# A decoder layer on one Trainium2 core: early bounds on ScalarE, the second head's weights loaded early, the weight-sum product inside pair 3, the last row's tiles stored apart

## What is computed

```python
# 1. attention with decay: 16 heads of 128, q, k, v = split(silu(x @ Wqkv.T))
out = per head: (q k^T * decay(i - j), for i >= j) @ v        # slope per head
out = out * rsqrt(mean(out * out) + eps) * norm_w
y = (sigmoid(x @ Wg.T) * out) @ Wo.T
x = layernorm(x + y)
# 2. WKV recurrence over time, with keys x and values ctx_2048
x = layernorm(x + wkv(time_decay, time_first, x, ctx))
# 3. feed-forward with ternary weights
w_hat = sign(round(w / (mean(|w|) + eps))) * mean(|w|)         # for w_fc and w_proj
h = gelu(bitlinear(x, w_fc)); x = layernorm(x + bitlinear(h, w_proj))
```

## Time and profile before

| | us |
|---|---|
| median of three runs | 1334.83 |
| lowest, highest | 1333.92, 1334.94 |
| profiled execution, its own time | 1334.65 |
| its span in the profile | 1332.9 |
| mean granted TensorE clock | 0.995 |
| busy: TensorE, VectorE, ScalarE, GpSimd | 1289.5, 967.8, 629.6, 298.2 |

### The profile page before, as it was taken

How to read it: one execution, slowest core, us unless ns; L and a number is a source line. 1 busy time by engine, 2 the same in 40 slices (tenths; PEclk the granted TensorE clock), 3 DMA queues, 4 the chain that set the end, 5 groups by cost and what they waited for, 6 DMA issues and landing times.

```text
span 1332.9 us, 20153 instructions
## 1 busy us (share of the span) xinstructions
PE 1289.5 (97%) x7468; PEld 830.8 (62%) x7468; DVE 967.8 (73%) x1882; ACT 629.6 (47%) x1138; POOL 298.2 (22%) x213
## 2 busy tenths in 40 slices
PE   5899999999999999999999999999998999999997
PEld 3566666666666666666666666666665555555553
DVE  6875776696577667766776677667678788998763
ACT  3443343344333433533353344334356678888854
POOL 2112111111110111111111111111125565555630
PEclk9999999999999999999999999999999999999999
DMA  5100021121111111011111110001010111110000
GB/s 186 60 17 16 25 88 32 48 80 64 33 65 32 48 32 41 24 49 32 40 53 36 32 49 32 32 16 41 1 48 17 33 32 48 48 48 32 17 17 32
DMA packets 19103, 55.83 MB, mean 42 GB/s; under 512 B 2624, under 2 KB 2624, under 8 KB 18624
## 3 DMA queue, kind: packets, MB, share of 16 engines
q1 hardware_dynamic: 19008, 54.55, 12.3%
HBM read 50.35 MB, written 4.19 MB: 41 GB/s over the span
## 4 chain that ended last, share of the span: by engine, by line
PE 59%; DVE 5%; ACT 3%; issue 2%; POOL 1%; ACTq 0%; POOLq 0%; DVEq 0%
PE bank L399 7%; PE bank L400 7%; PE bank L401 7%; PE bank L613 4%; PE bank L614 4%; PE bank L471 3%; PE bank L473 3%; PE bank L472 3%; PE bank L414 3%; PE bank L416 2%; PE bank L415 2%; PE bank L639 2%; PE bank L638 2%; PE bank L459 1%; PE bank L442 1%
## 5 line engine op out<-in xcount | busy, mean ns | idle before, releaser
L399 PE MATMUL bank<-x_hi,w_hi 128*128 128x512 f16 x768 | 294.6, 384 | 5.2 <-DVE w_lo L1076 2.9
L1122 DVE TENSOR_TENSOR resid<-resid,bank 128x512 f32<-128x512 f32 x256 | 173.2, 686 | 173.5 <-PE bank L473 172.9
L400 PE MATMUL bank<-x_lo,w_hi 128*128 128x512 f16 x768 | 293.8, 383 | 0.0
L401 PE MATMUL bank<-x_hi,w_lo 128*128 128x512 f16 x768 | 293.2, 382 | 0.0
L1578 POOL TENSOR_TENSOR sq_sum<-sq_sum,o_sq 128x512 f32<-128x512 f32 x64 | 106.6, 1665 | 797.0 <-ACT o_sq L757 797.0
L757 ACT ACTIVATE o_sq<-bank 128x512 f32<-128x512 f32 x64 | 38.3, 599 | 287.9 <-DVE gated L1128 287.9
L414 PE MATMUL bank<-wv_hi,x_hi 128*128 128x256 f16 x512 | 139.6, 273 | 1.0 <-DVE x_lo L1137 0.6
L416 PE MATMUL bank<-wv_hi,x_lo 128*128 128x256 f16 x512 | 139.6, 273 | 0.0
L415 PE MATMUL bank<-wv_lo,x_hi 128*128 128x256 f16 x512 | 139.6, 273 | 0.0
L399 PEld LDWEIGHTS bank<-x_hi,w_hi 128*128 128x128 f16 x768 | 76.5, 100 | 91.9 <-issue 19.9
L401 PEld LDWEIGHTS bank<-x_hi,w_lo 128*128 128x128 f16 x768 | 75.7, 99 | 92.5 <-issue 3.3
(11 more groups left out here) (174 smaller groups left out, 2660.2 us busy)
## 6 DMA issues: line engine op xcount, KB each, us to landing
w_raw<-w_ffn SPq DMA_DIRECT2D x32, 512.0 KB, 3.5
raw_a<-w_heads SPq DMA_DIRECT2D x32, 256.0 KB, 3.8
raw<-w_heads SPq DMA_DIRECT2D x15, 512.0 KB, 3.6
raw<-w_heads SPq DMA_DIRECT2D x18, 256.0 KB, 3.9
x_in<-x_rows SPq DMA_DIRECT2D x8, 512.0 KB, 3.8
out<-y_out SPq DMA_DIRECT2D x8, 512.0 KB, 2.6
resid<-x_t SPq DMA_DIRECT2D x3, 1024.0 KB, 8.0
val<-ctx_t SPq DMA_DIRECT2D x6, 512.0 KB, 3.5
```

The costliest lines, as they stand in the source:

```text
L399: mm(bk[:, :], a, c, start=kt == 0, stop=False)
L400: mm(bk[:, :], a, d, start=False, stop=False)
L401: last = mm(bk[:, :], b, c, start=False, stop=kt == KT - 1)
L1122: tt(resid[:, 4 * g + t, :], resid[:, 4 * g + t, :], YB[t % 2][:, :], ALU.add).then_inc(y_added, 1)
```

## The change

- ScalarE takes over bounds, as sums of magnitudes (`Abs` with an accumulated output) in place of maxima: K and G of head 0 (`sum_w`) ahead of x's high parts, V (`sum_v`) behind them, head 1's Q, K, G (`sum_w1`) between the split of q and the evacuation of K in unit 0, and x group 1 (`sum_x`) between the evacuations of G and V in unit 0. VectorE keeps the bounds of Q of head 0, x groups 0, 2 and 3, and all of the later pairs.
- TensorE does the K and G bound ahead of unit 0, the V bound behind project Q, and head 1's bound between the two V projections of unit 0. VectorE does the K and G scale ahead of x's low parts.
- Before and between the first bounds TensorE runs 8, 14 and 5 filler products of 128x512 on a matrix of ones, into a bank that nothing reads.
- `w_raw` grows to 1536 columns and takes head 1's weights of pair 0, loaded behind V's and ahead of x group 1; the first feed-forward chunk is loaded when they are split (`wsplit` 6).
- In units 1, 2 and 4 of pair 0 VectorE splits all four chunks of the next x group ahead of the additions and of k's split.
- The weight-sum product goes to unit 1 of pair 3, behind mix, into columns 416 and 417 of `SC[1]`; the thresholds are worked out behind VectorE's other work of that unit, ahead of gate; TensorE waits for them ahead of the second scores of unit 2.
- In the last row each tile has its own variance, root, shift, activation and store.

The diff, cut to its core:

```diff
 load_v(0, 1)
+sp.dma_start(w_raw[:, 0:2 * HID]..., w_heads[1, :, 0:2, :]).then_inc(w1_in, 16)
+sp.dma_start(w_raw[:, 2 * HID:3 * HID], w_heads[1, :, 3, :]).then_inc(w1_in, 16)
 load_x(1)
-sp.wait_ge(wsplit, PROJ)
-load_w(1)
...
-sp.dma_start(w_raw[:, :], w_ffn[0, :, :]).then_inc(fraw_in, 16)
...
+sp.wait_ge(wsplit, 2 * PROJ)
+sp.dma_start(w_raw[:, 0:CW], w_ffn[0, :, :]).then_inc(fraw_in, 16)
...
+for t in range(BT):
+    sp.wait_ge(last_out[t], 1)
+    sp.dma_start(out[BATCH - 1, :, t, :], y_out[:, t, :]).then_inc(stored, 16)
+sp.wait_ge(stored, 16 * (BATCH + 1))
# TensorE
                     scores(u - 1, 0)
+                    if p == TERN_PAIRS[0] and t == 2:
+                        pe.wait_ge(thr_ok, 6)
...
                 project(u, p, t, Q, first_pair)
                 if first_pair and t == 0:
-                    w_bound(2, K, V, (xbig_ok, 1))
+                    w_bound(3, V, V + 1, (winv_ok, 2))
...
                 project(u, p, t, K, first_pair)
-                if first_pair and t == 0:
-                    w_bound(3, V, V + 1, (winv_ok, 2))
...
+                if p == TERN_PAIRS[0] and t == 1:
+                    pe.wait_ge(abs_two_ok, 1)
+                    pe.wait_ge(masked, 2 * u)
+                    mm(GB, ones[:, :], abs_two[:, :], start=True, stop=True).then_inc(gamma_ok, 1)
...
                     project_v(0, 0, VB)
+                    w_bound(4, Q, V, (winv_ok, 3))
                     project_v(0, 1, YB[0])
-                    w_bound(4, Q, V, (winv_ok, 3))
...
+            def keep_busy(n):
+                for _ in range(n):
+                    mm(YB[1][:, :], ones16[:, :], ones16[:, 0:1].broadcast_to([P, 512]), start=True, stop=True)
+            pe.wait_ge(pool_const, 5)
+            keep_busy(8)
             pe.wait_ge(ident_ok, 1)
             w_bound(1, Q, K, None)
+            keep_busy(14)
             x_bound(0, (winv_ok, 1))
+            w_bound(2, K, V, (xbig_ok, 1))
+            keep_busy(5)
             pair(0, first_pair=True)
...
-            pe.wait_ge(abs_two_ok, 1)
-            pe.wait_ge(masked, 2 * (PER_PAIR * ABS_PAIRS[1] - 1))
-            mm(SC[0][:, 0:2], ones[:, :], abs_two[:, :], start=True, stop=True).then_inc(gamma_ok, 1)
-            pe.wait_ge(thr_ok, 6)
# ScalarE
+            def sum_w(j):
+                act.wait_ge(wraw_in, 32)
+                fn(v_all[...], raw[:, j, :], ACT.Abs, accum_out=wmax[:, j:j + 1]).then_inc(w_sum_ok, 1)
+            def sum_w1(j):
+                act.wait_ge(w1_in, 32)
+                act.wait_ge(wbound_ok, 2)
+                act.wait_ge(w_sum_ok, 3 + j)
+                fn(o_sq[:, :], w_raw[:, j * HID:(j + 1) * HID], ACT.Abs, accum_out=wmax[:, j:j + 1]).then_inc(w_sum_ok, 1)
+            def sum_v():
+                act.wait_ge(wv_in, 32)
+                fn(v_all[...], raw_a[...], ACT.Abs, accum_out=wmax[:, V:V + 1]).then_inc(w_sum_ok, 1)
+            def sum_x(kt):
+                act.wait_ge(xraw_in[KT], 16)
+                wait(act, x_sum_ok, kt)
+                fn(o_sq[:, :], resid[:, 4 + kt, :], ACT.Abs, accum_out=xmax[:, 1, kt:kt + 1]).then_inc(x_sum_ok, 1)
...
             decay(1, 1, 0)
+            sum_w(K)
+            sum_w(G)
             for kt in range(KT):
                 split_x(0, kt)
+            sum_v()
             pair(0, first_pair=True)
# VectorE
             dequant(0, 0, Q, K)
+            scale_w(2, 0, K, V)
+            dequant(0, 0, K, V)
             for kt in range(KT):
                 split_x(0, kt)
-            bound_w(2, 0, K, V)
-            scale_w(2, 0, K, V)
-            dequant(0, 0, K, V)
             split_w(0, 0, K, 2)
             split_w(0, 0, G, 2)
-            bound_v(0)
             scale_v(3)
...
-                if first_pair and t in (0, 1, 3):
+                if first_pair and t in (1, 3):
                     bound_x(1 + (t + 1) // 2, 0, KT)
...
                 def ternarise_chunk(t):
+                    if p == TERN_PAIRS[0] and t == 1:
+                        thresholds()
...
-            bn(NO, 1, y_out[:, 1, :])
-            variances(NO, LN_EPS)
-            shift(NO, BATCH - 1)
+            for t in range(BT):
+                if t:
+                    after(result(BATCH - 1, 1, 1))
+                    after(bn(NO, 1, y_out[:, 1, :]))
+                aggregate(NO, t)
+                ts(var_e[:, NO, t:t + 1], mv[:, NO, t, 1:2], LN_EPS, None, ALU.add).then_inc(last_var[t], 1)
+                dve.wait_ge(last_rstd[t], 1)
+                stt(nshift[:, NO, t:t + 1], mv[:, NO, t, 0:1], -1.0, rstd[:, NO, t:t + 1], ALU.mult,
+                    ALU.mult).then_inc(last_shift[t], 1)
```

More of the change, by code:

```diff
@@ L126, in decoder_layer @@
         raw_a = sb("raw_a", [P, 2, HID], F32, att)
[L127 to L128 removed]
+        w_raw = sb("w_raw", [P, CW + HID], F32, att)
         wv_hi = sb("wv_hi", [P, 2, KT, DH], F16, att)
@@ L240, in decoder_layer @@
         hq_turned, hqh_ok, hql_ok = sem("hq_turned"), sem("hqh_ok"), sem("hql_ok")
+        last_var, last_rstd = [sem(f"last_var{t}") for t in range(BT)], [sem(f"last_rstd{t}") for t in range(BT)]
+        last_shift, last_out = [sem(f"last_shift{t}") for t in range(BT)], [sem(f"last_out{t}") for t in range(BT)]
         col_done, col_ok = sem("col_done"), sem("col_ok")
@@ L376, in _ @@
             load_ctx(BATCH - 1)
-            for b in range(BATCH - 4, BATCH):
+            for b in range(BATCH - 4, BATCH - 1):
                 store(b)
-            sp.wait_ge(stored, 16 * BATCH)
+            for t in range(BT):
+                sp.wait_ge(last_out[t], 1)
+                sp.dma_start(out[BATCH - 1, :, t, :], y_out[:, t, :]).then_inc(stored, 16)
+            sp.wait_ge(stored, 16 * (BATCH + 1))
         @block.tensor
@@ L425, in w_bound @@
             def w_bound(k, j0, j1, after):
-                pe.wait_ge(wmax_ok, k)
+                if isinstance(k, int) and k in (2, 3, 4):
+                    pe.wait_ge(w_sum_ok, {2: 2, 3: 3, 4: 6}[k])
+                else:
+                    pe.wait_ge(wmax_ok, 1 if isinstance(k, int) and k == 1 else k - 3)
                 if after:
@@ L823, in unit @@
                         split_x(t // 2 + 1, kt)
+                if first_unit:
+                    for j in (Q, K, G):
+                        sum_w1(j)
                 evacuate(u, t, K, first_unit)
@@ L837, in unit @@
                 if first_unit:
+                    act.wait_ge(w_sum_ok, 6)
+                    for kt in range(KT):
+                        sum_x(kt)
                     evacuate_v(1, 1, 0, 0, 0, VB)
@@ L1173, in unit @@
                     dequant_v(gx)
-                    split_x(gx, 0)
-                    split_x(gx, 1)
+                    for kt in range(KT):
+                        split_x(gx, kt)
                 if lag2:
@@ L1538, in _ @@
             row(BATCH - 1, 1, next_row=False, second_row=False, third_row=False)
-            after(result(BATCH - 1, 1, 1))
-            bn(NO, 1, y_out[:, 1, :])
-            variances(NO, LN_EPS)
-            shift(NO, BATCH - 1)
+            after(steps.base + steps.n)
+            for t in range(BT):
+                if t:
[6 more added lines that the diff above has]
+                    ALU.mult).then_inc(last_shift[t], 1)
         @block.gpsimd
@@ L1722, in _ @@
             row(BATCH - 1, 1, next_row=False, second_row=False, third_row=False)
-            root(NO, BATCH - 1)
+            for t in range(BT):
+                pool.wait_ge(last_var[t], 1)
+                g_.tensor_tensor(rstd[:, NO, t:t + 1], var_e[:, NO, t:t + 1], neg_half[:, 0:1],
+                                 ALU.pow).then_inc(last_rstd[t], 1)
 def kernel(x, ctx_2048, L0_attn_slope_rate, L0_attn_Wqkv, L0_attn_Wg, L0_attn_norm_w, L0_attn_Wo,
```

68 lines of the change are left out of this document (40 added, 28 removed).

## The result

| | kernel before | changed kernel |
|---|---|---|
| median, runs | 1334.44 us, 4 runs (1333.92 to 1334.94) | **1319.40 us**, 4 runs (1318.53 to 1320.02) |
| ratio | | 0.9885 [0.9871, 0.9899] |
| profiled execution, its span | 1334.65, 1332.9 | 1319.16, 1317.4 |

The account below looks back on a forecast made before the run. TensorE, busy 1289.5 of 1332.9 us, was taken as the bound, so only shorter stops or low-clock stretches pay. 1334.65 - 8.9 (opening) - 5.0 (weight-sum product) - 1.7 (last row) = 1319.0 us, range 1316.8 to 1325.

Parts of the forecast that it names:

- The opening: Term for units 0 and 1 and the waits in later units of pair 0: -8.9 us, bounds -10.5 to -5.5.
- Mix waits a little for the split probabilities (34.3): Opening, unit 1: after K starts at 31.35, mix waits briefly until 34.3; G ends 38.2.
- 0.5 more: Opening: waits of 0.28 at 66.28 and its twin in unit 4 go, adding 0.5 us to the 8.4 ahead.
- Their data must be there by 10.2: Opening: K's and G's data needed by 10.2 for ScalarE's sums to stay hidden; arrival estimated at 9.5.
- a wait for ScalarE's sums at any bound: Listed sign, in the changed profile, that the prediction would be wrong; no size given.
- The middle: Weight-sum product moved from between pairs 2 and 3: stop and slow Q products go, -5.0 us, bounds -3.4 to -5.2.
- The last row: Kernel's end: less VectorE and ScalarE work and a smaller last store, -1.7 us, bounds -1.1 to -2.2.
- Fillers stay cold: Rival, opening: the 14 fillers end at 13.1 instead of 10.9, all behind 2.2 later: 1321.2 us, chance 0.14.
- Sums reload tables: Rival, ScalarE in unit 0: table changes cost 1.28 each, 5.1 in all, half absorbed: 1321.7 us, chance 0.07.
- VectorE is the bound of pair 0: Rival: VectorE's small waits in units 1 to 4 return half the opening's gain: 1323.5 us, chance 0.11.
- The stop is only moved: Rival: TensorE waits as long for the thresholds in unit 2 of pair 3: 1324.0 us, chance 0.03.
- Slower: Rival: fillers' gaps cost the higher clock level throughout units 0 to 2; full price gives 1352 us, chance 0.03.

Follow-up runs that it names:

- again: The changed kernel itself, unedited, run once more on the chip of the next three runs: 1319.93 us, ratio 0.9881.
- u_kgv: Changed kernel with K's, G's and V's bounds of head 0 as maxima on VectorE again, in their old places: 1321.48 us, ratio 0.9898.
- u_mid: Changed kernel with the weight-sum product and thresholds back between pairs 2 and 3: 1323.31 us, ratio 0.9911.
- u_tail: Changed kernel with the last row's common root, shift and single store back: 1320.52 us, ratio 0.9893.
- u_xsum: Changed kernel with the bound of x group 1 as a maximum on VectorE again: 1320.37 us, ratio 0.9888.
- u_load: Changed kernel with x group 1 loaded before head 1's weights, which wait until head 0's are split: 1319.97 us, ratio 0.9886.
- nofill: Changed kernel without its 27 filler products: 1320.95 us, ratio 0.9887.
- earlyw: Changed kernel with 4, 12 and 5 fillers in the opening instead of 8, 14 and 5: 1318.05 us, ratio 0.9868.
- best: Changed kernel with opening fillers 4, 15, 3 and 5, plus fillers in the late mix and in the stop behind the last pair: 1317.31 us, ratio 0.9865.
- both: Changed kernel with 4, 12 and 5 opening fillers and 12 fillers in the stop behind the last pair: 1317.47 us, ratio 0.9864.
- stopfill: Changed kernel with 12 filler products in the 2.84 us stop behind the last pair: 1317.66 us, ratio 0.9864.

## Why the prediction was right, and where its terms were off

**The opening, -8.9, measured -10.08.** Its chain held at each step: x's bound at 10.84 (10.9), Q at 13.46 (13.8), K at 16.55 (16.9) and 2.27 ahead where 1.9 were worked out, scores at 27.04 (27.4), head 1's bound product in V at 24.36 (24.7), Q of unit 1 at 28.27 (28.6), x's bound without a wait, the new wait for x_lo 0.75 (0.9). Mis-sized were two steps. "Mix waits a little for the split probabilities (34.3)": from K of unit 1 to the mix I had 2.95, measured 2.40 and no wait, which with the 0.35 won earlier makes the 0.86 by which V of unit 1 came sooner (38.24 for 39.1). And "0.5 more" for the waits at 66.28 and in unit 4: the gap in front of each was longer than the listed 0.28, and both together gave 0.82. Together 1.2: one small wait was forecast that did not come, and the two that went were longer than the list of idle times says.

"Their data must be there by 10.2" was met in every profile (the sums ran from 9.13 in the first, from 9.94 in again, from 10.03 at the latest), and yet it was the wrong test. It took x's bound at 10.9; where the level is granted sooner that bound is at 9.87, and then data of 9.94 is late: TensorE waits 1.07, and Q is slow. The prediction called a wait for ScalarE's sums at any bound a sign of being wrong, and again has it. u_kgv shows that moving these bounds was the right thing to put most of K's gain on. The clock of K's products was in the sum without being named: "K and G warm" carries the lead from 1.9 at K to 3.9 at the scores. Of the 1.5 that K of unit 1 saves in the same way, the prediction says "runs warm".

**The middle, -5.0, measured -5.07**, and -4.7 by u_mid. The thresholds reached VectorE at 415.63 to 416.3 and gate ran at 416.35; no TensorE instruction waited for them.

**The last row, -1.7, measured -1.93.** The steps were the right ones; the root, taken as unchanged at 0.70, takes 0.56 on one column, which is 0.14 of the 0.23.

**What was missing: +1.58 behind the last pair.** I took the stretch from pair 3 to the end as unchanged. Its work was, its clock was not: the fall of the level behind stops that were there before is what cancelled the 1.2, 0.1 and 0.2 that the other terms gave beyond their size. The profiled execution was forecast to 0.2 us (the median to 0.4) by this cancellation, which is luck; without the late loss the profiled execution would have come to 1317.6, 1.4 below the forecast. u_tail, u_xsum and u_kgv are such executions.

**The rivals.** *Fillers stay cold* did not happen in its form, since the level was granted during the fillers each time. Its effect, a Q at 1.2 GHz, did, by another way, in three of the eleven profiled executions whose opening has the changed kernel's bounds and some fillers (two of the eight with its own 8, 14 and 5): behind a wait for ScalarE's sums of about 1 us. The Trainium skill, TensorE: Matmul & The Clock Gate, in its part on the warm-up, says that the number of slow products at a start varies between runs of one kernel; the two openings of the changed kernel agree, 3.60 and 3.22 for the same eight fillers. *Sums reload tables* fell: the ten sums brought no load. (Its price adds up to 1321.6, not 1321.7.) The Trainium skill, ScalarE: Activation LUTs, on table sets, has abs in every set; the trace agrees, one load of 1.28 ahead of Silu and none around the sums at 17.90 and 22.52. *VectorE is the bound of pair 0* fell: from K of unit 0 to pair 3 TensorE's timeline has one wait of over 0.1 us behind K's own, the 0.75 for x_lo, where the kernel before had four (0.82, 2.94, 0.28, 0.28). *The stop is only moved* fell with the thresholds at 416.3. *Slower* fell; in pair 0 the level was back within one projection in every execution.

**What stays open.** In which executions the level falls behind a given stop. u_tail, u_xsum and u_kgv had the late stops of the changed kernel in their old form, and no loss (891.07 to 891.13), as the kernel before (891.10); the first profile, u_mid, u_load, nofill, earlyw and again had the loss. No edit separates the two lists, and none of these edits touches that stretch. Nor is it proven that fillers prevent the fall. At the last stop it fell in none of four profiles with fillers, and in four of ten without; at the late mix in neither of the two with fillers, and in eight of twelve without. And about 3 us of the opening's gain belong to no part that was undone.

## What to carry to other kernels

Look for the reduction in front of a product chain that an idle engine could do: the largest part of the opening's gain that was measured, 4.3 of 10.1, came from taking three bounds (K, G and V) out of VectorE's queue, and it was worth its wait plus the slow products behind that wait. A stop of a few microseconds on TensorE has two prices, its length and, in some executions, 1.2 to 1.7 us of products at half clock; in the six places where cheap products into a free bank reached up to the end of such a late wait, the second was not paid. A fall of the level can also cost nothing, where TensorE would have waited a little later anyhow. Read a part's worth in its own stretch between two fixed marks, because a whole-kernel median mixes in clock losses elsewhere that are as large as the part.

## What the runs showed of the hardware that was not expected

- The same stop, two outcomes: 2.84 idle behind the last pair is followed by products 0.43 apart in one execution (1025.90) and 0.23 apart in another of the same kernel (1028.08). The late stretch takes 891.06 to 891.13 or 892.28 to 892.72, with nothing between.
- More work can be faster: best issues 32 products more than the changed kernel and is 2.6 us shorter in the medians run together; and fillers that reach the full level sooner end sooner, which opened a wait (1.07) that the slower ones had covered, and the level fell 1.35 behind its end.
- A fall of the level has no fixed price: behind the late mix, slow products cost 0 in the first profile, u_mid, u_load, earlyw and both, and 1.2 to 1.3 in again, nofill and stopfill, where they were more than a later wait of 1.46 absorbs.
- A sum over 128x512 on ScalarE takes one slot of about 0.82 us with its accumulator read (three of them start at 17.90, 18.72 and 19.55), against 0.85 worked out; over 128x1024, 1.04 and 0.19.
- GpSimd's power took 0.56 us on one column against 0.70 on two.
